# Fused attention and experts on one core: the causal mask moves from TensorE into VectorE's maximum, and the transposed scores of two heads become row tiles with one exponential

## What is computed

```python
Q = rope((x @ qw).reshape(batch, seq, n_heads, n_dim), freq)   # the same for K with kw; V has no rope
score = jnp.einsum('bhqd,bhkd->bhqk', Q, K) / scale
causal = jnp.tril(jnp.ones((1, 1, seq, seq), dtype=jnp.float32))
score = score - 10000000000.0 * (1.0 - causal)
score = score - jnp.max(score, axis=-1, keepdims=True)
weights = jax.nn.softmax(score, axis=-1)
attn = jnp.einsum('bhqk,bhkd->bhqd', weights, V)
...
x = _layernorm(x + attention(x))
x = _layernorm(x + experts(x))
```

## Time and profile before

| | us |
|---|---|
| median of 3 runs | 498.72 (497.11 to 499.74) |
| span of the profiled execution | 495.2 |

### The profile page before, as it was taken

How to read it: one execution, slowest core, us unless ns; L and a number is a source line. 1 busy time by engine, 2 the same in 40 slices (tenths; PEclk the granted TensorE clock), 3 DMA queues, 4 the chain that set the end, 5 groups by cost and what they waited for, 6 DMA issues and landing times.

```text
span 495.2 us, 10480 instructions
## 1 busy us (share of the span) xinstructions
PE 463.4 (94%) x2676; PEld 296.0 (60%) x2676; DVE 323.8 (65%) x802; ACT 285.1 (58%) x594; POOL 166.9 (34%) x167
## 2 busy tenths in 40 slices
PE   5779999999999999999999999989999999999992
PEld 2346555555554654655655545447887787787781
DVE  3879757777677676777776774313656756756743
ACT  1311146765766766767657666956565565565560
POOL 4524010230411402402304112126645564564661
PEclk9986579999999999999999999999999999999997
DMA  7877411212112112202121000000000000000000
GB/s 249 267 226 192 122 21 26 68 33 66 40 19 64 40 19 64 57 18 67 37 65 39 3 1 3 2 0 1 1 1 3 21 0 0 21 0 0 22 0 22
DMA packets 41738, 23.49 MB, mean 47 GB/s; under 512 B 31280, under 2 KB 33968, under 8 KB 41712
## 3 DMA queue, kind: packets, MB, share of 16 engines
q1 hardware_dynamic: 41712, 23.18, 17.1%
HBM read 14.26 MB, written 8.65 MB: 46 GB/s over the span
## 4 chain that ended last, share of the span: by engine, by line
PE 77%; DVE 7%; issue 4%; ACT 4%; DMA 4%; SPq 3%; POOL 1%; DVEq 0%; ACTq 0%; POOLq 0%
PE bank L960 20%; PE bank L975 15%; PE bank L1044 14%; PE bank L938 14%; PE bank L1055 7%; DVE maxima L703 2%; PE bank L993 2%; DMA k_scratch<-rope_lo 2%; PE bank L941 2%; ACT num L600 1%; DVE num L763 1%; DVE num L836 1%; ACT num L539 1%; SPq L314 1%; PE bank L1020 1%
## 5 line engine op out<-in xcount | busy, mean ns | idle before, releaser
L539 ACT ACTIVATE num<-bank 128x512 f32<-128x512 f32 (+3 forms) x384 | 168.8, 495 | 101.6 <-PE bank L960 99.1
L703 DVE TENSOR_REDUCE maxima<-bank 128x1 f32<-128x512 f32 (+15 forms) x384 | 182.3, 519 | 66.9 <-PE bank L941 46.2
L960 PE MATMUL bank<-q_op,k_op 128*128 128x512 f32 (+3 forms) x384 | 148.2, 419 | 2.8 <-ACT num L539 1.7
L938 PE MATMUL bank<-k_op,q_op 128*128 128x512 f32 (+15 forms) x384 | 126.3, 369 | 3.4 <-issue 2.9
L437 POOL TENSOR_SCALAR_AFFINE_SELECT num<-num 128x512 f32<-128x512 f32 x64 | 40.6, 635 | 226.0 <-ACT num L539 224.1
L960 PEld LDWEIGHTS bank<-q_op,k_op 128*128 128x128 f32 x384 | 71.4, 197 | 69.1 <-ACT num L539 62.0
L468 POOL TENSOR_TENSOR q_op<-num,q_op 128x512 fp32r<-128x512 f32 x64 | 82.4, 1290 | 63.6 <-ACT q_op L593 60.3
L938 PEld LDWEIGHTS bank<-k_op,q_op 128*128 128x128 f32 x384 | 77.0, 202 | 19.2 <-DVE maxima L703 10.9
L1044 PE MATMUL bank<-q_op,w_hi 128*128 (+1 forms) x256 | 81.9, 401 | 1.7 <-DVE num L836 1.6
L975 PE MATMUL bank<-num,v_op 128*32 128x512 f32 (+3 forms) x768 | 82.5, 503 | 0.0
L836 DVE TENSOR_TENSOR num<-bank,num 128x512 f32<-128x512 f32 x64 | 44.2, 691 | 58.5 <-ACT num L600 54.8
(11 more groups left out here) (86 smaller groups left out, 315.7 us busy)
## 6 DMA issues: line engine op xcount, KB each, us to landing
k_op<-k_scratch SPq DMA_DIRECT2D x16, 256.0 KB, 2.7
q_op<-q_scratch SPq DMA_DIRECT2D x64, 52.0 KB
w_raw<-in_w_all SPq DMA_DIRECT2D x6, 512.0 KB, 4.3
q_scratch<-rope_hi SPq DMA_DIRECT2D x8, 256.0 KB, 3.1
k_scratch<-rope_hi SPq DMA_DIRECT2D x8, 256.0 KB, 3.6
xT<-in_x_feat SPq DMA_DIRECT2D x4, 256.0 KB, 6.1
k_scratch<-k_op SPq DMA_DIRECT2D x2, 512.0 KB, 6.2
q_scratch<-rope_lo SPq DMA_DIRECT2D x4, 256.0 KB, 3.9
```

The lines of the kernel that those rows point to most:

```text
L539: act.activation(num[:, t % PB, h, off:CH], t_bank[k % TB][:, off:CH], ACT.Exp, scale=scale)\
L703: dve.tensor_reduce(maxima[:, half, j:j + 1], s_bank[k % SB][:, 0:width], AX.X, ALU.max)\
L938: ins = pe.matmul(s_bank[k % SB][:, 0:width], q_op[u][:, j, :, :].rearrange("p h q -> p (h q)"), k_op[u][:, lo:lo + width], start=True, st ...
L960: pe.matmul(t_bank[k % TB][:, off:CH].rearrange("p (j q) -> p j q", q=QD), k_op[w][:, kt * P:(kt + 1) * P], q_op[w][:, c * NB + off // QD: ...
```

## The change

The mask leaves TensorE. mask_b, ident_b, their two copies on ScalarE and the matmul of L941 are gone. VectorE builds a strip `causal` of 512 columns (480 zeros by a memset, the last 32 from the mask in DRAM) and, for a unit that touches the diagonal, adds the strip's last `width` columns to the bank and takes the maximum in one instruction, `tensor_tensor_reduce`; the sum itself goes to a scratch tile that nobody reads. Units without a diagonal keep tensor_reduce.

The T units are halved in number: a unit is one kt and two heads. Each head has a matmul of its own 32 partitions (tile_position (32 head, 0)) into its own bank, and one exponential reads both banks. The banks are dealt anew: two for S (SB = 2), two pairs for T (TB = 2), o_bank and small_bank as before. The numbers that place MROWS, NORM and the C steps follow the new count of units. The V projection and the rotation use the same bank numbers under new names.

```diff
@@ -33,32 +33,34 @@
+LOWEST = -3e38
...
-T_UNITS = [(c, kt, h) for c in range(NC) for kt in range(TI * (c + 1)) for h in range(GH)]
+HP = GH // 2
+T_UNITS = [(c, kt, h) for c in range(NC) for kt in range(TI * (c + 1)) for h in range(HP)]
...
-NPV = NT // GH
-SB = 3
-TB = 3
+NPV = NT // HP
+SB = 2
+TB = 2
...
-MROWS_AT, NORM_AT, MROWS0_AT, NORM0_AT = 5, 12, 19, 25
+MROWS_AT, NORM_AT, MROWS0_AT, NORM0_AT = 2, 6, 9, 12
...
-        s_bank, t_bank, o_bank, small_bank = bank[0:3], bank[3:6], bank[6], bank[7]
+        s_bank = [ctx.enter_context(nc.psum_tensor(f"s_bank{i}", [P, CH], F32)) for i in range(SB)]
+        t_bank = [ctx.enter_context(nc.psum_tensor(f"t_bank{i}", [P, 2, CH], F32)) for i in range(TB)]
...
+        causal, masked_s = resid, (mg_w, mg_t, x1_w)
...
+            sp.wait_ge(causal_cleared, 1)
+            for dst, src in ((ident[:, :], ident_d), (causal[:, CH - QD:CH], mask_d)):
...
-                        act.activation(num[:, t % PB, h, off:CH], t_bank[k % TB][:, off:CH], ACT.Exp, scale=scale)\
+                        act.activation(num[:, t % PB, 2 * h:2 * h + 2, off:CH], t_bank[k % TB][:, :, off:CH], ACT.Exp, scale=scale)\
...
+            dve.memset(causal[:, 0:CH - QD], 0.0).then_inc(causal_cleared, 1)
...
-                        dve.tensor_reduce(maxima[:, half, j:j + 1], s_bank[k % SB][:, 0:width], AX.X, ALU.max)\
-                            .then_inc(s_reduced, 1)
+                        if QD * (j + 1) - lo <= CH:
+                            if k == 0 and plan is PROLOGUE:
+                                dve.wait_ge(ld_small, 16 * 2)
+                            dve.sem_inc(dve_turn, 1)
+                            dve.tensor_tensor_reduce(masked_s[k % SB][:, 0:width], s_bank[k % SB][:, 0:width],
+                                                     causal[:, CH - width:CH], 1.0, LOWEST, ALU.add, ALU.max,
+                                                     maxima[:, half, j:j + 1]).then_inc(s_reduced, 1)
+                        else:
+                            dve.tensor_reduce(maxima[:, half, j:j + 1], s_bank[k % SB][:, 0:width], AX.X, ALU.max)\
+                                .then_inc(s_reduced, 1)
...
-                        ins = pe.matmul(s_bank[k % SB][:, 0:width], q_op[u][:, j, :, :].rearrange("p h q -> p (h q)"),
-                                        k_op[u][:, lo:lo + width], start=True, stop=not diagonal)
-                        if diagonal:
-                            ins = pe.matmul(s_bank[k % SB][:, width - QD:width], ident_b[:, :], mask_b[:, :],
-                                            start=False, stop=True)
-                        ins.then_inc(s_ready, 1)
+                        pe.matmul(s_bank[k % SB][:, 0:width], q_op[u][:, j, :, :].rearrange("p h q -> p (h q)"),
+                                  k_op[u][:, lo:lo + width], start=True, stop=True).then_inc(s_ready, 1)
...
-                        pe.matmul(t_bank[k % TB][:, off:CH].rearrange("p (j q) -> p j q", q=QD),
-                                  k_op[w][:, kt * P:(kt + 1) * P],
-                                  q_op[w][:, c * NB + off // QD:(c + 1) * NB, h, :], start=True, stop=True)\
-                            .then_inc(t_ready, 1)
+                        for i in range(2):
+                            head = 2 * h + i
+                            rows = slice(head * QD, (head + 1) * QD)
+                            ins = pe.matmul(t_bank[k % TB][:, i, off:CH].rearrange("p (j q) -> p j q", q=QD),
+                                            k_op[w][rows, kt * P:(kt + 1) * P],
+                                            q_op[w][rows, c * NB + off // QD:(c + 1) * NB, head, :],
+                                            start=True, stop=True, tile_position=(head * QD, 0))
+                        ins.then_inc(t_ready, 1)
```

More of the change, by code:

```diff
@@ L53 @@
 C_STEPS = 15
-C_FROM, C_EVERY = 4, 3
+C_AT = [2 + 3 * r // 2 for r in range(C_STEPS)]
 PROJ_FIRST = 6
@@ L60 @@
 S_LATE, S_EARLY = 0, 3
-MROWS_AT, NORM_AT, MROWS0_AT, NORM0_AT = 5, 12, 19, 25
+MROWS_AT, NORM_AT, MROWS0_AT, NORM0_AT = 2, 6, 9, 12
 def stage_plan(with_s, with_t):
     s_units = S_UNITS if with_s else []
-    t_units = [(u, 0) for u in T_UNITS[GH:]] if with_t else []
-    t_units += [(u, 1) for u in T_UNITS[:GH]] if with_s else []
+    t_units = [(u, 0) for u in T_UNITS[HP:]] if with_t else []
+    t_units += [(u, 1) for u in T_UNITS[:HP]] if with_s else []
     def s_work(units):
@@ L94, in stage_plan @@
         plan.append(("T", c, kt, h, ahead))
-        if not with_s and at >= C_FROM and (at - C_FROM) % C_EVERY == 0 and (at - C_FROM) // C_EVERY < C_STEPS:
-            plan.append(("C", (at - C_FROM) // C_EVERY))
+        if not with_s and at in C_AT:
+            plan.append(("C", C_AT.index(at)))
         part = min(1, t_work(t_units[S_LATE:x + 1]) / max(1, t_work(t_units[S_LATE:len(t_units) - S_EARLY])))
@@ L100, in stage_plan @@
             done_s += 1
-        if h == GH - 1 and with_t and not with_s:
-            t = at // GH - 2
+        if h == HP - 1 and with_t and not with_s:
+            t = at // HP - 2
             if t >= 0:
@@ L107, in stage_plan @@
                 plan.append(("OCOPY", 0))
-        elif h == GH - 1 and with_t:
+        elif h == HP - 1 and with_t:
             if kt >= 1:
@@ L168, in sem @@
             return ctx.enter_context(nc.semaphore(name))
-        bank = [ctx.enter_context(nc.psum_tensor(f"bank{i}", [P, CH], F32)) for i in range(8)]
-        s_bank, t_bank, o_bank, small_bank = bank[0:3], bank[3:6], bank[6], bank[7]
+        s_bank = [ctx.enter_context(nc.psum_tensor(f"s_bank{i}", [P, CH], F32)) for i in range(SB)]
+        t_bank = [ctx.enter_context(nc.psum_tensor(f"t_bank{i}", [P, 2, CH], F32)) for i in range(TB)]
+        o_bank, small_bank = (ctx.enter_context(nc.psum_tensor(n, [P, CH], F32)) for n in ("o_bank", "small_bank"))
+        bank = [*s_bank, *(t[:, i, :] for t in t_bank for i in range(2)), o_bank, small_bank]
         q_dram = nc.dram_tensor("q_scratch", (B * H, QROWS, S), F32).ap()
@@ L429, in stage @@
                     _, c, kt, h, ahead = step
-                    if kt >= TI * c and h == GH - 1:
+                    if kt >= TI * c and h == HP - 1:
                         k = NT * ahead + T_UNITS.index((c, kt, h))
```

21 lines of the change are left out of this document (6 added, 15 removed).

## The result

The changed kernel takes 692.64 us, median of 4 (682.57 to 697.12), where before takes 498.69 on the same chip: a ratio of 1.377, 95% interval 1.367 to 1.387. The forecast was 545 us with a range to 588. The sign was right; 194 us came where 46 were forecast.

A forecast was written before the change was run, and what follows sets the result against it. TensorE was taken to bound seven steady stages of 34.0 us. Span 495.2 + 40 (stages) + 6 (prologue) + 0 (last stage) = 541 us, plus 3.5 between span and measured median: 545 us, own range 520 to 565, overall 500 to 588.

The forecast's parts named there:

- rival B: Steady stages: TensorE's clock falls, 15 us more a stage at half clock, a third of the time; 580 us, chance 0.15.
- The stage at full clock: Steady attention stage: 39.7 us against 34.0 before, 5.7 us more per stage, 40 us over seven.
- Two banks: Score units in steady stages: third S waits until the first bank is reduced, delaying T and PV; the term that decides.
- The block that I worked: One attention block, two T pairs and five S units before PV, worked: 4.15 us against 3.16 before.
- T pairs: Transposed scores on TensorE: 0.44 us per 512-wide pair with shape changes; 0.24 without their price, 0.65 if not overlapping.
- The masked maximum: VectorE's diagonal units: two instructions, w/960 + 0.20 us for w columns, 3.8 us more VectorE time per stage.
- my low end: Masked maximum on VectorE: the second instruction hides, so a unit of w columns costs w/960 + 0.08 us.
- The mask matmuls: TensorE, 32 per stage: removal saves 0.12 us each, 3.8 us per stage, 27 us if nothing else changed.
- Prologue and last stage: Before and after the steady stages: two banks add 6 us to the prologue; last stage 0, between -2 and +3.
- C (faster): Steady stages: VectorE's chain and TensorE overlap, a stage takes 31 us; 480 us in all, chance 0.12.
- D (half-speed maximum): VectorE: masked maximum runs at half speed, 5.7 us more a stage; 585 us in all, chance 0.06.
- A: Steady stages: small prices at low ends, T pair 0.24 us, second instruction hidden; stage 34.5 us, total 504 us, chance 0.17.

The follow-up runs named there:

- run with single tiles: Kernel before with each T matmul a row tile of 32 rows, three S and three T banks, mask on TensorE: 779.99 us, ratio 1.565.
- unrolled mask kernel: Kernel before with the mask on VectorE and the loop over steady stages written out on all five engines: 488.47 us, ratio 0.980.

## Why the prediction was wrong

**The step that failed: the clock.** The sum took every steady stage at clock 1.00 and left the clock to rival B, with a chance of 0.15 and a third of the time at half clock. It was most of every steady stage: 0.55 was granted over six stages (98.05 to 462.45 us), nine tenths of the time at half clock. B's mechanism was right, and its price per stage (15 us) was near what the windows show (63.0 against 43.8, 19 us); its extent was the error. I had argued from the last stage before, which held 1.00 with little work, but every matmul in it was fed over 128 rows. The run with single tiles shows what few rows did, the one with one bank what waits did. The last stage of the changed kernel has tiles but no S units, and from its first PV on it was granted 0.84 in the short part and 0.82 in the long one; why, no run tells.

**The stage at full clock**: forecast 39.7 us, estimate from the traces 43.8, without tiles 42.1 measured. The seven stages took 186 us more than before where the sum had 40. Of the 146 us that were missing, seven times 4.1, 29 us, are the stage at full clock, and the other 117 are by this estimate the clock, with the two gaps at the jumps in it. Prologue and last stage, below, add 8 us, and that is the whole miss of the span: 541 forecast, 695.3 measured.

**Two banks**: right in mechanism. Alone they cost 4.6 us a stage, and 40 us in all with the prologue. The block that I worked, 4.15 us at full clock, took 4.46 from PV to PV in the kernel without tiles (102.69 to 107.15), and the fifth S waited for VectorE. TensorE there, order of time:

```profile
102.69 1.07 PE L982 MATMUL o_bank<-num,v_op 128*32 128x512 f32 x8
103.68 0.74 PE L966 MATMUL t_bank<-q_op,k_op 128*128 128x512 f32 x2
104.27 0.55 PE L945 MATMUL s_bank<-k_op,q_op 128*128 128x512 f32 x2
104.66 0.63 PE L966 MATMUL t_bank<-q_op,k_op 128*128 128x512 f32 x2
105.44 0.88 PE L945 MATMUL s_bank<-k_op,q_op 128*128 128x512 f32 x2
106.72 0.50 PE L945 MATMUL s_bank<-k_op,q_op 128*128 128x512 f32 x1 [0.40 <-DVE maxima L712]
107.15 1.06 PE L982 MATMUL o_bank<-num,v_op 128*32 128x512 f32 x8
```

With pairs and the S units in a row it is 7.1 us a stage (41.1 less 34.0, full rows, mask on TensorE), where the sum had 5.7 for all parts of the change together.

**T pairs**: side by side, right (3 ns). The change of shape is 0.20 us each way, not 0.10 and 0.11, so a 512-wide pair costs 0.61 us (an estimate: 0.21 of streaming and two changes), near my high end of 0.65. The changes around PV, from which I took the price, are not the same: there the rows stay 128 and only the columns change. The Trainium skill's rule (TensorEngine Tiling (Array Packing), Key Properties), that a change of the tiling mode drains the array, agrees with the 0.20 us at full and 0.29 at half clock here.

**The masked maximum**: my low end was right. VectorE of the unrolled mask kernel, order of time:

```profile
115.77 0.41 DVE L705 CUSTOM_DVE_ANT_0 mg_t<-bank,resid 128x256 f32<-128x256 f32 x1
116.11 0.08 DVE L705 DVE_READ_ACCUMULATOR2_ANT maxima<- 128x1 f32 x1
116.11 0.69 DVE L709 TENSOR_REDUCE maxima<-bank 128x1 f32<-128x512 f32 x1
```

256 columns, and the next instruction starts 0.34 us later, together with the read: w/960 + 0.07, the price of a plain reduction. The small aggregates were the wrong row. Two instructions per unit were right, and their length in the program, not their time, is what cost.

**The mask matmuls**: booked at 27 us, worth 11. I had read 0.32 against 0.24 us as their price on the T behind them. The reading was right (without the mask a T behind an S takes 0.24 in the median), but only 20 of the 32 in a stage have a T behind them, and what TensorE gains there is lost again in waits. The waits of T's weight loads for ScalarE, 7.4 us a stage before, were in the trace and not in my reading: "TensorE is busy 94%" made me take it for a pure bound.

**Prologue and last stage**: forecast +6 and 0. The first PV comes 12.4 us later in the changed kernel and 10.8 later with two banks alone (75.1 us), so the prologue's term was half of what it should be, and the banks are most of it. The last stage takes 24.7 us from its first PV to its last (505.1 to 529.8), 23.4 before (306.4 to 329.8): +1.3. Its head, from the last S unit to that first PV, is counted in the seventh stage above and is another 3.6 us longer (6.9 before, 10.5 after, at clock 0.50). With it the last stage is outside my -2 to +3, and again by the clock.

**Rivals**: C (faster) and D (half-speed maximum) didn't occur. A's price of the second instruction was right, its price of the tiles was not.

## What to carry to other kernels

Before narrowing matmuls to row tiles, count how often they alternate with full-row ones: each change cost 0.15 to 0.20 us here, nearly what 512 columns stream (0.21), and the granted clock of the stretch fell to half even where TensorE hardly ever waited. Feeding zeros over all 128 rows, which looks like waste, kept the full clock with two S banks and the mask on TensorE, though not where TensorE waited more. Before an edit that lengthens an engine's instruction list inside a loop, look for the gap at the jump back; writing the loop out turned the same edit from 1.5% slower into 2% faster.

## What the hardware showed that I had not expected

- Matmuls over 32 of 128 rows between full-row ones: clock 0.50 for 437 us of attention (88.96 to 525.71 us) with TensorE busy throughout. With 64 rows the same program switched between 0.50 and 0.98 from one part to the next, and from one execution to another (667 to 783 us).
- A change between full-row and 32-row matmuls: 0.20 us at full clock, 0.29 at half; with 64 rows 0.15 on average; between full-row matmuls of 128 and 32 columns (S to PV) 0.09.
- A loop's jump back on VectorE: 3.5 to 3.9 us in which it stands still once its body has grown (3.85 and 3.61 with the mask alone, 3.46 in the changed kernel); with the shorter body of before, parts with a jump are 0.3 to 0.4 us longer than the others (23.0 and 23.1 against 22.7).
- An addition and maximum in one, with its accumulator read, takes VectorE no longer than the maximum alone (256 columns: 0.34 us to the next start).
